# One DMA in place of four for the rows of an expert unit, with the row numbers' DMA moved to SyncE

## The reference

```python
logits = jnp.einsum('bsd,de->bse', x, Wg)
P = jax.nn.softmax(logits, axis=-1)
_, topk_idx = jax.lax.top_k(P, K)                       # K = 2 of E = 8
mask = jax.nn.one_hot(topk_idx, E, dtype=x.dtype).sum(-2)
P_norm = P * mask / ((P * mask).sum(axis=-1, keepdims=True) + EPS)
h = jax.nn.gelu(jnp.einsum('bsd,edf->ebsf', x, W1) + b1[:, None, None, :], approximate=False)   # F = 512
y_e = jnp.einsum('ebsf,efd->ebsd', h, W2) + b2[:, None, None, :]
y = jnp.einsum('ebsd,bse->bsd', y_e, P_norm)
```

## Time and profile before

| | us |
|---|---|
| median of 3 runs | 447.39 (444.95 to 447.6) |
| profiled execution | 445.98 |
| its span | 444.2 |
| PE busy | 405.7 (91%) |
| DVE busy | 305.1 (69%) |
| ACT busy | 199.8 (45%) |
| POOL (GpSimd) busy | 156.5 (35%) |

### The profile page before, as it was taken

One profiled execution on the slowest core, in us unless ns is written; L12 is line 12 of the kernel. 1 busy time (PEld: TensorE's weight loads), 2 busy tenths in 40 slices (PEclk: granted clock), 3 DMA queues, 4 the chain that ended last, 5 costly groups with the idle time before them and its releaser, 6 DMA issues.

```text
span 444.2 us, 10450 instructions
## 1 busy us (share of the span) xinstructions
PE 405.7 (91%) x2870; PEld 341.6 (77%) x2870; DVE 305.1 (69%) x1174; ACT 199.8 (45%) x488; POOL 156.5 (35%) x215
## 2 busy tenths in 40 slices
PE   8699989999999999999988898886999999999963
PEld 7579777878869779787767787775899999999521
DVE  4889889888888878878867667622456555555327
ACT  3364555565554545543524243231444455554212
POOL 6340015013233250344434011443555555465400
PEclk9999999999999999999999999999899999999968
DMA  7449611254056231132222423422444444442665
GB/s 185 120 111 154 73 40 36 56 164 136 19 135 186 58 82 38 47 83 53 60 64 52 74 53 83 101 82 42 72 78 75 78 78 84 77 88 48 220 218 172
DMA packets 105013, 40.83 MB, mean 92 GB/s; under 512 B 68868, under 2 KB 97928, under 8 KB 104968
## 3 DMA queue, kind: packets, MB, share of 16 engines
q1 hardware_dynamic: 90480, 31.20, 32.4%
q0 software_dynamic: 4352, 8.99, 6.0%
q10 hardware_dynamic: 10136, 0.10, 1.3%
HBM read 21.78 MB, written 18.48 MB: 91 GB/s over the span
## 4 chain that ended last, share of the span: by engine, by line
PE 61%; DVE 20%; issue 7%; DMA 4%; ACT 4%; POOL 1%; SPq 1%; ACTq 1%; DVEq 0%; POOLq 0%
PE psA L1042 12%; PE psC L1053 11%; PE psB L875 7%; PE psB L863 5%; DVE stats L1352 2%; PE psB L1064 2%; DMA results<-nat,y_to 2%; PE psD L992 2%; DVE nt_a L1367 1%; POOL routed L714 1%; DVE nt_a L1366 1%; PE psB L865 1%; DVE rstd L1368 1%; PE psA L821 1%; PE psB L895 1%
## 5 line engine op out<-in xcount | busy, mean ns | idle before, releaser
L714 POOL DMA_INDIRECT routed<-send,slot x64 | 65.3, 1020 | 128.5 <-DMA routed<-send,slot 55.5
L723 POOL DMA_INDIRECT results<-nat,y_to x72 | 69.9, 971 | 85.6 <-DVE nat L1677 69.7
L1246 ACT ACTIVATE h1T<-psA,b1T 128x256 f32<-128x256 f32 x144 | 63.1, 474 | 65.8 <-PE psC L1053 49.1
L1042 PE MATMUL psA<-xuT,w_all 128*128 128x256 f32 x288 | 69.1, 383 | 2.8 <-issue 1.5
L1042 PEld LDWEIGHTS psA<-xuT,w_all 128*128 128x128 f32 x288 | 51.0, 191 | 10.3 <-issue 2.4
L1053 PEld LDWEIGHTS psC<-w_all,h1T 128*128 128x128 f32 x464 | 56.3, 192 | 2.2 <-ACT h1T L1246 0.8
L1053 PE MATMUL psC<-w_all,h1T 128*128 128x128 f32 x464 | 56.6, 275 | 0.6 <-ACT h1T L1246 0.6
L863 PE MATMUL psB<-xnT,w_l 128*128 128x512 f32 x64 | 34.4, 618 | 0.0
L875 PE MATMUL psB<-w_l,hg0T 128*128 128x128 f32 x256 | 32.7, 281 | 0.2 <-ACT hg0T L1181 0.2
L1181 ACT ACTIVATE hg0T<-psB,b1T 128x512 f32<-128x512 f32 x32 | 22.0, 688 | 22.8 <-PE psB L865 22.7
L875 PEld LDWEIGHTS psB<-w_l,hg0T 128*128 128x128 f32 x256 | 31.2, 192 | 1.1 <-ACT hg0T L1181 0.6
(11 more groups left out here) (287 smaller groups left out, 833.3 us busy)
## 6 DMA issues: line engine op xcount, KB each, us to landing
ring<-routed SPq DMA_DIRECT2D x152, 32.0 KB
inv<-inv_room SPq DMA_DIRECT2D x8, 512.0 KB, 4.1
w_all<-results SPq DMA_DIRECT2D x15, 256.0 KB, 5.0
routed<-ring SPq DMA_DIRECT2D x24, 130.0 KB, 7.5
n_room<-nT SPq DMA_DIRECT2D x8, 256.0 KB, 2.5
w_all<-in_L_ffn_W_dram SPq DMA_DIRECT2D x1, 2048.0 KB, 9.6
out_dram<-x_all SPq DMA_DIRECT2D x8, 256.0 KB, 2.3
results<-nat,y_to POOLq DMA_INDIRECT x72
```

The source lines that it names most:

```text
L714: pool.indirect_dma_start(routed[:, :], bass.IndirectOffsetOnAxis(ap=slot[par][:, c, t:t + 1], axis=0), send[par][:, c, t, :], None).then_ ...
L723: pool.indirect_dma_start(results[:, :], bass.IndirectOffsetOnAxis(ap=y_to[:, par, a:a + 1], axis=0), yw[:, par, a, :], None).then_inc(S[f ...
L1042: last = mm(psA[:, j // 2, (j % 2) * UNIT:(j % 2 + 1) * UNIT], w1_all[:, e, j * P:(j + 1) * P], xuT[:, :], start=True, stop=True)
L1246: f(h1T[:, j, :], psA[:, j // 2, (j % 2) * UNIT:(j % 2 + 1) * UNIT], ACT.Gelu, bias=b1T[:, n:n + 1]).then_inc(S["gelu_ready"], 1)
```

## The change

The four DMAs of a unit become one, whose destination takes whole partitions of the ring (128 x 256 floats) and whose source is walked column piece by column piece: the dimensions of the source are 4 pieces, 256 rows, 32 floats. With that, row p*8+b of the unit (it was row b*32+p) stands in column b*32+p of the turned tile. One semaphore, `unit_in`, takes the place of the two, and a load is issued when the load before it has landed. The DMA of the row numbers is issued by SP right behind the load of the rows, and no longer by ACT; ACT no longer waits for the rows of the last group, nor works out addresses. The Gelu writes its 256 columns with a step of 4 floats, so that the rows of a result stand as the row numbers do (row 2m+a of the unit on partition m, half a).

```diff
             def load_unit(u, row):
+
+                wait_on(sp, "unit_in", u * 16)
+                sp.sem_inc(apart, 1)
                 if not isinstance(u, int) or u >= RING:
                     wait_on(sp, "xu_ready", u - RING + 1)
                     sp.sem_inc(apart, 1)
-                at = bass.ds(u % RING, 1)
-                rows = routed[bass.ds(row, UNIT), :]
-                for c in range(PIECES):
-                    name = UNIT_IN[c // 2]
-                    if c % 2 == 0:
-                        wait_on(sp, name, u * PAIR_IN)
-                    sp.dma_start(ring_x[c * BLOCK:(c + 1) * BLOCK, at, :]
-                                 .rearrange("p r (b e) -> p (r b) e", e=BLOCK),
-                                 rows[:, c * BLOCK:(c + 1) * BLOCK]
-                                 .rearrange("(b p) e -> p b e", p=BLOCK)).then_inc(S[name], 16)
+                sp.dma_start(ring_x[:, bass.ds(u % RING, 1), :],
+                             routed[bass.ds(row, UNIT), 0:P].rearrange("r (c e) -> c r e", e=BLOCK)
+                             ).then_inc(S["unit_in"], 16)
+
+            def load_to(u, row):
+
+                wait_on(sp, "to_in", u * 16)
+                sp.sem_inc(apart, 1)
+                wait_on(sp, "ring_free", u - TO_RING + 1)
+                sp.dma_start(ring_iw[:, bass.ds(u % TO_RING, 1), :, :].rearrange("p r a w -> p (r a) w"),
+                             routed[bass.ds(row, UNIT), COL_ID:].rearrange("(m a) w -> m a w", a=HALVES)
+                             ).then_inc(S["to_in"], 16)
...
                 with sp.Fori(bounds[e], bounds[e + 1]) as u:
-                    load_unit(u, unit_row(u, e, bounds))
+                    row = unit_row(u, e, bounds)
+                    load_unit(u, row)
+                    load_to(u, row)
...
-                    f(h1T[:, j, :], psA[:, j // 2, (j % 2) * UNIT:(j % 2 + 1) * UNIT], ACT.Gelu,
+                    f(h1T[:, j, :].rearrange("h (m b) -> h b m", b=TURNS),
+                      psA[:, j // 2, (j % 2) * UNIT:(j % 2 + 1) * UNIT].rearrange("h (b m) -> h b m", b=TURNS), ACT.Gelu,
                       bias=b1T[:, n:n + 1]).then_inc(S["gelu_ready"], 1)
-
-            def load_to(u, row):
-
-                wait_on(act, "to_in", u * 16)
-                act.sem_inc(apart, 1)
-                wait_on(act, "ring_free", u - TO_RING + 1)
-                act.dma_start(ring_iw[:, bass.ds(u % TO_RING, 1), :, :].rearrange("p r a w -> p (r a) w"),
-                              routed[bass.ds(row, UNIT), COL_ID:].rearrange("(a p) w -> p a w", p=P)
-                              ).then_inc(S["to_in"], 16)
...
             def take(u):
 
-                for name in UNIT_IN:
-                    wait_on(dve, name, (u + 1) * PAIR_IN)
-                    dve.sem_inc(apart, 1)
+                wait_on(dve, "unit_in", (u + 1) * 16)
+                dve.sem_inc(apart, 1)
```

More of the change, by code:

```diff
@@ L65 @@
 BLOCK = 32
-PIECES = P // BLOCK
-UNIT_IN = ("left_in", "right_in")
-PAIR_IN = 32
+TURNS = P // BLOCK
 SLOT = P // TILES
@@ L382, in two_block_kernel @@
             "s1_ready",
-            *UNIT_IN, "to_in",
+            "unit_in", "to_in",
             "ring_free",
@@ L395, in two_block_kernel @@
         )}
-        SEEDED = {"yb_ready": 1, "y_landed": 2, **{name: 1 for name in UNIT_IN}, "to_in": 1, "ring_free": TO_RING, "xu_ready": RING, "h1_free": JF,
+        SEEDED = {"yb_ready": 1, "y_landed": 2, "unit_in": 1, "to_in": 1, "ring_free": TO_RING, "xu_ready": RING, "h1_free": JF,
                   "gelu_ready": JF, "yw_ready": 1}
@@ L494, in _ @@
                                  ring[:, n + 1 if n else e % 2, :, :]).then_inc(prefilled, 16)
-            for name in UNIT_IN:
+            for name in ("unit_in", "to_in"):
                 sp.sem_inc(S[name], SEEDED[name])
             def load_unit(u, row):
+                wait_on(sp, "unit_in", u * 16)
+                sp.sem_inc(apart, 1)
                 if not isinstance(u, int) or u >= RING:
@@ L569, in unit_work @@
                         sp.sem_inc(apart, 1)
-                    load_unit(k, k % E * REGION + k // E * UNIT)
+                    row = k % E * REGION + k // E * UNIT
+                    load_unit(k, row)
+                    load_to(k, row)
             first_pass(sp, work, unit_work)
@@ L578, in _ @@
                 with sp.Fori(bounds[e], bounds[e + 1]) as u:
-                    load_unit(u, unit_row(u, e, bounds))
+                    row = unit_row(u, e, bounds)
+                    load_unit(u, row)
+                    load_to(u, row)
             load_unit(bounds[E], 0)
             load_unit(bounds[E] + 1, 0)
-            for name in UNIT_IN:
-                wait_on(sp, name, (bounds[E] + 2) * PAIR_IN)
-                sp.sem_inc(apart, 1)
+            wait_on(sp, "unit_in", (bounds[E] + 2) * 16)
+            sp.sem_inc(apart, 1)
+            wait_on(sp, "to_in", bounds[E] * 16)
+            sp.sem_inc(apart, 1)
             def load_results(c, to, signal):
@@ L1111, in _ @@
             act.sem_inc(S["gelu_ready"], SEEDED["gelu_ready"])
-            act.sem_inc(S["to_in"], SEEDED["to_in"])
             def normalise(to, g, rstd, shift, first, signal):
@@ L1245, in gelus @@
                     wait_on(act, "h1_free", (u - 1) * JF + j + 1)
-                    f(h1T[:, j, :], psA[:, j // 2, (j % 2) * UNIT:(j % 2 + 1) * UNIT], ACT.Gelu,
+                    f(h1T[:, j, :].rearrange("h (m b) -> h b m", b=TURNS),
+                      psA[:, j // 2, (j % 2) * UNIT:(j % 2 + 1) * UNIT].rearrange("h (b m) -> h b m", b=TURNS), ACT.Gelu,
                       bias=b1T[:, n:n + 1]).then_inc(S["gelu_ready"], 1)
-            def load_to(u, row):
-                wait_on(act, "to_in", u * 16)
-                act.sem_inc(apart, 1)
-                wait_on(act, "ring_free", u - TO_RING + 1)
-                act.dma_start(ring_iw[:, bass.ds(u % TO_RING, 1), :, :].rearrange("p r a w -> p (r a) w"),
-                              routed[bass.ds(row, UNIT), COL_ID:].rearrange("(a p) w -> p a w", p=P)
-                              ).then_inc(S["to_in"], 16)
-            def hid(u, e):
-                load_to(u, unit_row(u, e, bounds))
             def out(u, f, e):
@@ L1265, in unit_work @@
             def unit_work(what, k=0):
[L1266 to L1271, removed]
+                if what == "gelu":
                     gelus(0, 0)
@@ L1279, in _ @@
             first_pass(act, work, unit_work)
[L1280 to L1286, removed]
+            other_units(act, bounds, lambda u, e: None, out)
             f(silu_first[:, :], b1T[:, 0:1], ACT.Silu)
```

## The result

The changed kernel took **495.02 us** (median of 4 runs, 494.0 to 495.81), the kernel before 447.38 us beside it. The ratio is **1.1105** (95% interval 1.1054 to 1.1157). The profiled execution has a span of 494.1 us, where it was 444.2 us. So the change costs 49.9 us of span.

A forecast was written before the change was run, and what follows sets the result against it. PE bounded the loop at 3.51 us a unit; a load cut 4 ways would become the pace at 5.9 us. 445.98 + 70.3 (loop) + 11.2 (ahead of it) - 1.5 (end) = 526.0 us, range 503 to 562 us.

The forecast's parts named there:

- Rival 1: Load's DMA cut 16 ways after all, PE the pace again: 445 us, 453 with the Gelu's upper bound; chance 0.06.
- Rival 2: Loop: idle PE's clock falls to 1.2 GHz, a unit costs PE 7.0 us: 559 us in all; chance 0.05.
- Rival 3: Load: four engines drain slower each, 20 ns a packet, period 7.5 us: 574 us in all; chance 0.08.
- the term for the load: Loop: one 4-way load takes 5.55 us; with SP's step a period of 5.9 us, +70.3 us over 30 loads.
- the one for the drain: Sign: the drain is wrong if the load takes far from 5.5 us with 4 completions.
- Packets, 3.55 us: Load in the loop: 257 packets on each of four engines at 13.8 ns, 3.55 us.
- Interference, 0.3 us: Load in the loop: other queues' results and row numbers on the same engines add 0.3 us.
- The fixed part, 1.7 us: Load: the part of a DMA that is not packets, 1.7 us (1.6 to 2.3), from line L529.
- SP's step, 0.35: Loop: SP's way from a released wait to issuing the next load, 0.35 us a unit.
- Ahead of the loop: Inside ORDER: longer loads delay group 7's scatters and the loop's first load, +11.2 us (8 to 13).
- The end: After the last take: only unit 34's output is already done, -1.5 us (0 to 3 saved).
- The rest, at nothing: ACT's lost issues, SP's second DMA and the Gelu's stepped write: hidden beside the load, no time.

The follow-up runs named there:

- e10: Changed kernel with the Gelu writing its columns in order, as before; ratio 1.1122 to the kernel before.
- e14: Kernel before with only the Gelu's output written with a step of 4 floats, run again; ratio 1.0184.
- e15: Changed kernel with each load bringing 128 of a unit's 256 rows, run again; ratio 1.0217 to the kernel before.
- e7: Changed kernel with a unit's load as two DMAs of two column pieces each; ratio 1.2818 to the kernel before.
- e2: Changed kernel with the DMA of the row numbers issued by ACT as before; ratio 1.0835 to the kernel before.
- e5: Changed kernel itself, unedited, measured again where the kernel before takes 462 us; ratio 1.0887.
- e13: Kernel before with only the order of the rows changed in its four DMAs, run again; ratio 1.0479.
- e12: Changed kernel with the load put back into four DMAs, new row order kept, run again; ratio 1.1182 to the kernel before.
- e1: Changed kernel with the load put back into four DMAs, new row order kept; ratio 1.0977 to the kernel before.
- e3: Kernel before with only the Gelu's output written with a step of 4 floats; ratio 1.0175.
- e4: Kernel before with only the DMA of the row numbers moved from ACT to SP; 477.7 us, ratio 1.0325.
- e6: Changed kernel with each load bringing 128 of a unit's 256 rows; 457.98 to 467.61 us beside 461.55, too scattered for a ratio.
- e8: Kernel before with only the order of the rows changed in its four DMAs; ratio 1.0557.
- e9: Kernel before itself, unedited, measured and profiled again; 446 us, ratio 0.9991.

## Why the prediction came out as it did

**Right: the cause.** The cut into 4, the load as the pace, DVE waiting in every unit (2.8 us; 2.4 forecast), the clock at 1.00. PE was busy for 80% rather than 60%, in part because the unit is shorter than forecast, in part because its products take more time of their own (with the plain Gelu, e10, it is 59.80 of 80 us, 75%). The loop's first load at 313.59 us lies within its 312 to 320. Rival 1 (the one meant where the prediction says "the second rival" of the coalescing rule) is dead by the count of completions. What it would have been worth was not run; e14 and e15, 454 to 455 us beside 446, speak for its upper value for the Gelu (453), not for 445. Rival 2 didn't come, although e7 shows that it is real one step further: with PE busy for 128.4 of 200 us the granted clock fell to 0.86. Rival 3 pointed the wrong way, as each of the four engines drains faster than I took, not slower.

**Wrong: the term for the load, "1.7 + 3.55 + 0.3 = 5.55 us", and with it the period of 5.9 us.** The period is 5.09 us, below the 5.4 that I gave as the lower end, and a load is taken 5.0 us after its issue. Of the prediction's own signs, it is the one for the drain that shows. Piece by piece:

- *Packets, 3.55 us.* I took the duration of a packet, 13.8 ns, for the distance of two. The loads' steady stretch shows the distance (DMA of the changed kernel, 249.3 to 251.7 us, load 0 alone; 40 slices, share in tenths and GB/s):

```profile
DMA  0333333333333333333333333333333333334578
GB/s 11 53 53 53 55 51 58 53 55 53 53 55 55 51 58 53 55 53 53 55 55 51 58 53 55 53 53 55 55 51 58 53 55 53 53 55 57 54 63 60
```

54 GB/s from four engines is 13.5 GB/s each, so 128 bytes every **9.5 ns**. 256 of them take 2.4 us, not 3.55. e7 and e15 agree with it from outside: 256 packets more cost 2.6 us a unit, 128 less saved 1.4 to 1.2 us, which is 9 to 11 ns a packet. In the same stretch the share of busy time (36.6% of 16 engines for 2.4 us, over 1128 packets) makes 12.5 ns a packet. So a packet's own duration is longer than the distance to the next, packets overlap on their engine, and in the earlier trace rows a share of busy time divided by a count of packets is a duration and no pace. This is 1.1 us of the error.
- *Interference, 0.3 us.* None is seen in the packets. From the issue to the last packet's end it is 4.16 us for load 0, with nothing beside it, and 4.14 us at the median of the loop.
- *The fixed part, 1.7 us, and SP's step, 0.35.* Their sum of 2.05 was too small: it is 5.09 - 2.4 = 2.7 us, though SP issues 0.05 us after DVE's take. Load 0 is taken 4.63 us after its issue (247.61 to 252.24); less 2.4 that leaves 2.2 us. In its packets' times 1.46 us of that lie before the first packet; in the kernel before, load 0 has 0.96. In the loop issue to take is 5.0 (median), so another 0.4 us pass after the last packet. That isn't explained: e2, with no DMA of row numbers on SP, has takes no closer (5.26 us; e5 has 5.17). The term came from the nearest row, 16-way with 32 packets a part, and it is 0.5 to 0.9 us more in a DMA of this form.

Together -1.1 - 0.3 + 0.6 or so: 5.1 us. Over 30 units 0.8 us are the 24.4 us by which the loop came out lower (+45.9, not +70.3).

**Ahead of the loop: +11.2 forecast, +8.0 measured.** The steps held almost to the end: take 2 at 261.74 (262.1 forecast), load 5 issued at 279.60 (279.7), taken at 286.02 (286.8), take 6 at 290.76 (292.2). Part of it is luck: load 0 itself began 1.3 us late, which I had not foreseen and which made up for loads that were shorter. Missing was that delay shrinks on its way: the first scatter is 8.9 us late behind a take that is 9.8 late, and the four pairs of scatters, each of which waits for the landing of the one before, gave back 0.8 us more.

**The end: -1.5 forecast, -4.0 measured.** PE begins the last sums 12.7 us after the last take instead of 14.9, which is my term at 2.1 us, within its 0 to 3. The rest I had missed, as it comes from a clock that was low before; the same sums and their window in the kernel before:

```profile
427.03 3.78 PE L1103 MATMUL psD<-w_all,ident 128*128 128x512 f32 x4 [3.73 <-DMA w_all<-results]
430.61 3.14 PE L1103 MATMUL psA<-w_all,ident 128*128 128x512 f32 x4
```

```profile
427.00:437.00 10.00, 9.97 (x16) 4.00 (x16) 6.48 (x10) 3.96 (x7) 0.00 (x0) 0.69 0.76 243
```

PE had idled for 3.73 us, and its first four products then took 3.78 us at a clock of 0.69 over the window; now it idles for 1.39 us, and they take 1.98 us. Over 478 to 487 us the clock is 1.00. From the first of these products to the end of the span it is 15.3 us instead of 17.2, which gives back the other 1.8 us.

**"The rest, at nothing"** held: e10 for the Gelu behind a long load, e2 for SP's second DMA. But both are free only under this load. In the kernel before, with a loop that is full on PE and nearly full on SP, each costs: 1.018 and, where that kernel takes 462 us, 1.03. The order of rows, which the prediction did not price at all, costs 1.048 there through SP's issues.

## What to carry to other kernels

One DMA in the place of four had a quarter of the parts, and with one load in flight at a time that decided: count the completions before believing in it. Price its packets by the bytes per second of a steady stretch, not by the packet's duration. And where a queue engine has only 0.4 us to spare in a unit, a change of the address pattern that leaves bytes and packets as they are can become the bound by its issue time; look at the issuing engine's own sum in a unit (here 3.09 of 3.51 us) before adding to it.

## What was unexpected of the hardware

- The duration of an issue on SP depends on the pattern: 326 ns for 32 partitions x 8 rows with rows 32 apart, 596 ns for the same with neighbouring rows (e13), 642 ns for the whole unit in one DMA.
- A DMA issued right behind the 4-part load holds SP far longer than its own issue. Line L513 of the changed kernel, and of e15, where that load has half as many packets:

```profile
L513 SPq DMA_DIRECT2D ring_iw<-routed x36: 1887/2196/4085, 248.4 to 451.7; - x36
```

```profile
L513 SPq DMA_DIRECT2D ring_iw<-routed x36: 664/916/2788, 247.6 to 413.6; - x36
```

Behind four 16-part DMAs it takes 0.61 us (e12). 128 packets a part less shorten the hold by 1.3 us, about what they take to drain. That it waits for room behind that load would fit, and was not tested.
- ScalarE writes 256 columns with a step of 16 bytes in 702 ns, in order in 473 ns: 0.9 ns a column more.
- Plain register instructions of SP stood for up to 0.7 us at a time (29 ns at the median) in e1, e3, e4, e6 and e8, and the kernel before took 3% longer beside those runs. The longest in e9 to e15 is 45 ns (310 to 400 us). What stops them isn't shown.
